# Two-layer decoder on one core: the first two queries of each cross-attention made in the stage ahead of it

## What is computed

```python
x = x + _L0_attn_ref(_layernorm(x), ...)            # softmax self-attention, 8 heads of 64
x = x + _L0_xattn_ref(_layernorm(x), ctx, ...)      # q = x Wq + bq, 16 heads of 16, softmax over 375 keys
x = x + _L0_ffn_ref(_layernorm(x), ...)             # top 2 of 8 experts, gelu, 1024 wide
x = x + _L1_attn_ref(_layernorm(x), ...)            # gated attention: norm again inside, silu, relu squared
x = x + _L1_xattn_ref(_layernorm(x), ctx, ...)      # norms x and the context with own gains and biases
x = x + _L1_ffn_ref(_layernorm(x), ...)             # top 2 of 8 experts, relu squared, 512 wide
```

## Time and profile before

| what | value |
|---|---|
| median of 3 runs | 2876.21 us (2872.34 to 2879.39) |
| profiled execution, its own time | 2876.75 us |
| its span | 2874.9 us |
| TensorE matmul busy | 2575.8 us, 90% of the span |
| VectorE busy | 1529.1 us, 53% |
| ScalarE busy | 1122.1 us, 39% |
| mean granted TensorE clock | 0.946 of full |

### The profile page before, as it was taken

The page is one execution under the profiler, slowest core; times in us unless marked ns, Lnnn a source line. Parts: engine busy times, 40 slices in busy tenths (PEclk is TensorE's granted clock), DMA queues, the critical chain, the costliest instruction groups (busy, mean ns, idle before and its releaser), DMA issues. The chain is left out here.

```text
span 2874.9 us, 57394 instructions
## 1 busy us (share of the span) xinstructions
PE 2575.8 (90%) x19210; PEld 2037.6 (71%) x19210; DVE 1529.1 (53%) x3357; ACT 1122.1 (39%) x2398; POOL 599.6 (21%) x652
## 2 busy tenths in 40 slices
PE   7999979789999975999999799899799999579992
PEld 4555555478888864888888566566688888468881
DVE  6777756456766664000000288455577777643334
ACT  2333345345555540333333244222455555312220
POOL 0000000023333310222222100000233333125542
PEclk9999999989999987999999899899899999779995
DMA  5110157777777732555555699000588888226666
GB/s 146 45 29 25 29 174 263 273 194 192 186 189 190 188 93 74 192 192 192 192 192 188 191 343 308 29 1 1 136 204 209 204 203 206 73 93 210 206 208 188
DMA packets 288417, 463.56 MB, mean 161 GB/s; under 512 B 75074, under 2 KB 216228, under 8 KB 288276
## 3 DMA queue, kind: packets, MB, share of 16 engines
q1 hardware_dynamic: 271508, 412.45, 50.3%
q0 software_dynamic: 16768, 49.30, 5.3%
HBM read 342.60 MB, written 119.02 MB: 161 GB/s over the span
## 5 line engine op out<-in xcount | busy, mean ns | idle before, releaser
L1444 ACT ACTIVATE x_probT<-banks 125x448 f32<-125x448 f32 x768 | 418.0, 544 | 382.9 <-PE banks L1341 372.8
L1544 DVE TENSOR_REDUCE x_neg_max<-banks 112x2 f32<-112x750 f32 x512 | 455.4, 930 | 93.4 <-PE banks L1325 93.4
L2103 PE MATMUL banks<-f_xT,f_w 128*128 128x256 f32 (+1 forms) x1680 | 369.9, 377 | 21.8 <-DMA f_b<-in_L_ffn_b 8.6
L2103 PEld LDWEIGHTS banks<-f_xT,f_w 128*128 128x128 f32 x1680 | 310.6, 197 | 74.9 <-issue 11.1
L1490 POOL TENSOR_TENSOR x_diag<-ident,x_neg_max 112x448 fp32r<-112x448 f32 x256 | 240.9, 941 | 581.6 <-DVE x_neg_max L1544 550.6
L2115 PE MATMUL banks<-f_w,f_hT 128*128 128x256 f32 x1584 | 355.8, 381 | 0.0
L1339 PE MATMUL banks<-x_diag,x_ones 112*125 112x448 f32 x768 | 324.0, 422 | 0.7 <-ACT x_probT L1444 0.6
L2115 PEld LDWEIGHTS banks<-f_w,f_hT 128*128 128x128 f32 x1584 | 297.7, 192 | 37.6
L1341 PEld LDWEIGHTS banks<-x_qP,x_kP 128*125 128x125 f32 x1536 | 290.5, 189 | 14.9
L1341 PE MATMUL banks<-x_qP,x_kP 128*125 128x224 f32 x1536 | 290.6, 271 | 0.0
L2162 DVE TENSOR_TENSOR f_y<-banks,f_b 128x256 f32<-128x256 f32 x66 | 25.1, 420 | 475.7 <-PE banks L2115 475.7
(11 more groups left out here) (331 smaller groups left out, 3789.1 us busy)
## 6 DMA issues: line engine op xcount, KB each, us to landing
x_kP<-k_halves SPq DMA_DIRECT2D x512, 188.0 KB, 3.6
f_w<-in_L_ffn_w SPq DMA_DIRECT2D x70, 1024.0 KB
f_w<-in_L_ffn_w SPq DMA_DIRECT2D x70, 512.0 KB
x_qP<-q_halves SPq DMA_DIRECT2D x512, 56.0 KB, 3.2
x_v<-v_rows SPq DMA_DIRECT2D x64, 408.0 KB, 3.2
k_halves<-p_halves SPq DMA_DIRECT2D x32, 752.0 KB, 4.5
k_halves<-f_d_halves SPq DMA_DIRECT2D x32, 752.0 KB, 6.4
q_halves<-x_q_halves SPq DMA_DIRECT2D x64, 224.0 KB, 2.3
```

The costliest lines, as they stand in the source:

```text
L1444: act.activation(probT[:, u % 2, c].rearrange("k h t -> k (h t)"), ST[i % 2][0:KB, 0:HU * T], ACT.Exp).then_inc(exp_done, 1)
L1544: dve.tensor_reduce(mx[:, u % RING, 2 * pair:2 * pair + 2], psum[0:T, 2 * pair:2 * pair + 2, 0:NKV], AX_X, ALU.max, negate=True).then_inc( ...
L2103: last = pe.matmul(bank[1 + f % 3][:, 0:width], w1[:, r, k, f * P:(f + 1) * P], xT[:, r, k, 0:width], start=(k == 0), stop=(k == KD - 1))
```

## The change

- The key stage's `KEYS` are four banks instead of two in layer 0, so that TensorE waits for VectorE's L1037 of the context two back (`least(2 * i + 2 - len(KEYS))`).
- `fold_pe` and the five bias additions go into the routing part of `experts(0)`; the nine weight scalings go one or two at a time ahead of VectorE's work of the last five expert tiles of layer 0.
- `first_queries` is new: it norms, turns, projects, splits and stores the queries of sequences 0 and 1 together. For layer 0 it stands in the key stage: factors and norm after context 26, TensorE's part behind the last context. For layer 1 it stands in `gated_attention`: factors of the two sequences and norm in group 4, TensorE's and ScalarE's part within the last group, VectorE's split ahead of the last group's `gated`.
- `cross_attention` starts its counters as if two queries had been made, and its opening loads keys and the stored queries at once. In layer 0 the norm factors are no longer made there.
- The two sets of norm factors of `gated_attention` are made at the end of layer 1's key stage.

```diff
@@ context_writer
     TURN, KEYS = (bank[0], bank[1]), (bank[2], bank[3])
+    if layer == 0:
+        KEYS = bank[0:4]
-        pe.wait_ge(k_low, ONE + 2 * i)
+        pe.wait_ge(k_low, ONE + least(2 * i + 2 - len(KEYS)))
@@ first_queries (new)
+    def norm(dve):
+        for b in range(2):
+            last = dve.tensor_scalar(xn[:, b, :], x[:, b, :], mv[:, b, 0:1], rstd[:, b:b + 1],
+                                     ALU.subtract, ALU.mult)
+    def turn(pe, to):
+        for k in range(KD):
+            for b in range(2):
+                last = pe.transpose(to[:, (2 * k + b) * T:(2 * k + b + 1) * T], xn[:, b, k * P:(k + 1) * P],
+                                    ident[0:T, 0:T])
+    def project(pe, to):
+        for m in range(KD):
+            for k in range(KD):
+                last = pe.matmul(to[:, m * TWICE:(m + 1) * TWICE], a.wqh[:, k, m, :], xnT[:, k, :],
+                                 start=(k == 0), stop=(k == KD - 1))
+    def store(sp):
+        sp.wait_ge(q_ready, 3)
+        for r in range(2):
+            sp.dma_start(e.q_halves[r].rearrange("h l p t -> p (h l) t"), ...).then_inc(stored, 16)
@@ project_context
             def _(pe):
                 for i in range(B):
                     c.tensor(pe, i)
-                    if i == FOLD:
-                        e.fold_pe(pe, wide_ready, folded_ps)
+                c.keys_read(pe, B - 2)
+                first.turn(pe, bank[0])
+                first.project(pe, bank[1])
...
-                        dve.wait_ge(folded_ps, 1)
-                        e.fold_dve(dve, fold_chain)
+                    if i == X_ASK:
+                        e.make_rstd_dve(dve, chain, x_std, x_asked, mv, rstd[:], e.norm_tmp, False, e.stat6)
+                        first.norm(dve)
+                first.split(dve, bank[1])
@@ cross_attention, SyncE
-                for half in range(2):
-                    load_keys(0, 0, half)
-                store_query(0, 0)
-                load_values(0, 0)
...
+                for s in range(2):
+                    load_keys(0, s, 0)
+                    sp.wait_ge(zeroed, s + 1)
+                    load_query(0, s)
+                    load_keys(0, s, 1)
+                    load_values(0, s)
@@ gated_attention
                 def project(g):
+                    if g + 1 == NG:
+                        pe.wait_ge(first.q_ready, 1)
...
+                    if g == NEXT:
+                        e.make_rstd_dve(dve, next_chain, std3, asked3, mv[:, 0:2], rstd[:, 0:2],
+                                        e.norm_tmp[:, :, 0:2], True, e.stat6[:, 0:2])
+                        first.norm(dve)
```

More of the change, by code:

```diff
@@ new lines, in decoder, with fold_weight @@
+        SCALES = 1 + 4 * KD
+        def fold_weight(dve, i, fold):
+            g = xa[1].gb
+            if i == 4 * KD:
+                fold(dve.tensor_scalar(xa[1].wv_twice[:], xa[1].wv_twice[:], g[:, 5:6], None, ALU.mult))
+                return
+            k, which = divmod(i, 4)
+            n = P if k == 0 else C1
+            if which == 0:
+                fold(dve.tensor_scalar(w.in_[:, k, :], w.in_[:, k, :], w.ln_gb[:, k:k + 1], None, ALU.mult))
+            elif which == 1:
+                wqh = xa[1].wqh[:, k].rearrange("c h n -> c (h n)")
+                fold(dve.tensor_scalar(wqh, wqh, g[:, k:k + 1], None, ALU.mult))
+            elif which == 2:
+                wkh = xa[1].wkh[:, k].rearrange("c h n -> c (h n)")
+                fold(dve.tensor_scalar(wkh, wkh, g[:, 4 + k:5 + k], None, ALU.mult))
+            else:
+                wv = xa[1].wv[0:n, k, :]
+                fold(dve.tensor_scalar(wv, wv, g[0:n, 4 + k:5 + k], None, ALU.mult))
@@ L1073, in _ @@
                 c.sync(sp)
+                first.store(sp)
                 c.stored(sp)
+                first.all_stored(sp)
             @block.gpsimd
@@ L1105, in _ @@
                         e.make_rstd_act(act, c_std, c_asked, ctmp)
+                    if i == X_ASK:
+                        e.make_rstd_act(act, x_std, x_asked, e.norm_tmp)
+                first.copy(act, bank[0])
             @block.vector
@@ L1412, in group @@
                             project(g, GROUP - 1)
-                for s in range(2):
-                    for j in MAKE:
-                        job(0, s, j)
                 pe.wait_ge(made, 2)
@@ L1476, in group @@
                             copy_oT(g, GROUP - 1)
-                for s in range(2):
-                    copy_xT(0, s)
                 for r in range(2, GROUP):
@@ L1592, in group @@
                             add_y(g, GROUP - 1)
-                for s in range(2):
-                    norm_x(0, s)
-                    split_q(0, s)
                 for u in range(AHEAD):
@@ L1804, in _ @@
                     pe.wait_ge(xT_ready, ONE + NG * KD)
+                    if layer == 0:
+                        e.fold_pe(pe, FOLD, fold_ps)
                     for n in range(2 * B):
@@ L2000, in _ @@
                     link(dve.tensor_copy(goes[:], spare[:]))
+                    if layer == 0:
+                        dve.wait_ge(fold_ps, 1)
+                        e.fold_biases(dve, FOLD, Chain(dve, fold_chain))
         xT = tile_sb("xT", [P, 2, KD, SLOTS])
@@ L2148, in _ @@
             def _(dve):
+                scale = Chain(dve, scaled)
                 def tile(n, i, r):
                     width = halves(n) * P
+                    if layer == 0 and type(n) is int:
+                        for j in range(2 * (n - PAIRED + 1), min(e.SCALES, 2 * (n - PAIRED + 2))):
+                            e.fold_weight(dve, j, scale)
                     if layer == 1:
@@ L2228, in _ @@
                     if layer == 0:
-                        e.residual_stats(dve, b)
+                        last = e.residual_stats(dve, b)
+                if layer == 0:
+                    last.then_inc(all_stats, 1)
+                    dve.wait_ge(all_stats, 1)
+                    factors = Chain(dve, pre2)
+                    e.make_rstd_dve(dve, factors, std1, asked1, mv, e.rstd_ga[:], e.norm_tmp, False, e.stat6)
+                    e.make_rstd_dve(dve, factors, std2, asked2, mv, rstd[:], e.norm_tmp, True)
 def gated_attention(e):
@@ L2268, in gated_attention @@
         tail = flag("tail")
+        NEXT = NG // 2
         def least(n):
@@ L2275, in gated_attention, with _ @@
         with nc.Block() as block:
+            @block.sync
+            def _(sp):
+                first.store(sp)
+                first.all_stored(sp)
             @block.tensor
@@ L2363, in _ @@
                         turn_in(g + 1)
+                    else:
+                        pe.wait_ge(y_read, ONE + g * GROUP)
+                        first.turn(pe, bank[0])
                     value(g, 2)
@@ L2504, in _ @@
                         queries_keys(g + 1)
+                    else:
+                        first.split(dve, bank[1])
                     for m in range(NE):
                         gated(g, m)
+                    if g == NEXT:
+                        next_chain = Chain(dve, next_pre)
+                        e.make_rstd_dve(dve, next_chain, std3, asked3, mv[:, 0:2], rstd[:, 0:2],
+                                        e.norm_tmp[:, :, 0:2], True, e.stat6[:, 0:2])
+                        first.norm(dve)
                     for s in range(GROUP):
```

149 lines of the change are left out of this document (92 added, 57 removed).

## The result

| | before | after |
|---|---|---|
| median of 3 runs | 2876.21 us | 2825.47 us (2824.13 to 2828.09) |
| profiled execution, its own time | 2876.75 us | 2828.09 us |
| its span | 2874.9 us | 2826.4 us |
| TensorE matmul busy | 2575.8 us | 2564.9 us |

The ratio is 0.983, with a 95% interval of 0.9815 to 0.9846: 1.7% faster. The prediction was 2828.

A forecast was written before the change was run, and what follows sets the result against it. TensorE was busy 90% of the span, so gains lay in its stalls and in work that could lie elsewhere. Terms -30, 0, +3.5, -10.2, -3.4, +3.0, -11.4 summed to -48.5 from 2876.75: forecast 2828 us, range 2818 to 2842.

The forecast's parts named there:

- Key stage, -30: Layer 0's key stage: removing the fold and adding two banks saves 30 us, bounds -32.4 to -13.3.
- The three kinds of loss: Key stage's 32.4 us lost: fold_pe near contexts 6 and 7, the hole after context 22, and remaining waits with lower-clock matmuls.
- kind (c): Key stage: 12.1 us of waits when finish or first factors held up VectorE, and lower-clock matmuls behind context 22's hole.
- the first rival: Key stage: stores pace it, by DMA rate or landing, so the kernel takes 2831 to 2845 us; chance 0.20.
- The estimate beside the forecast: Key stage: with HBM limited to about 358 GB/s, some 24 us come back in place of 30, 2834 in all.
- End of the key stage, +3.5: Border from key stage to stage 3: query work behind TensorE's end costs 3.5 us, bounds 0 to +6.
- Opening of stage 3, -10.2: First cross-attention: scores come 7.3 us after the stage's start instead of 17.5, saving 10.2 us.
- the second rival: Both cross-attention openings: other loads hold first scores or second key half 5 us each, kernel 2838 us; chance 0.12.
- The fold at 0: Routing and expert tiles of layer 0: the moved fold fits in TensorE's 18.78 us gap, costing 0, at worst +3.
- Gated attention's opening, -3.4: Border into gated attention: norm factors made before the stage begins save 3.4 us, range -1 to -4.
- Inside, +3.0: Gated attention: query transposes and products in the last group cost 2.1 us, VectorE work in group 4 costs 0.9.
- Opening of stage 6, -11.4: Second cross-attention: scores wait only for ones and query loads, 7.5 us after the start instead of 18.9, saving 11.4.

The follow-up runs named there:

- e1: Kernel after the change, but layer 0's key stage has two KEYS banks again instead of four: median 2838.35 us, ratio 0.9865 to before.
- e5: Kernel after the change, but layer 1's first two queries are made in the opening of cross-attention 1 (stage 6) again: median 2836.79 us.
- e6: Kernel after the change, but gated attention's two sets of norm factors are made at its opening again: median 2830.89 us.
- e7: Kernel after the change, but in both cross-attention openings ScalarE issues four of the first query load's eight DMAs, SyncE the other four: median 2827.26 us.
- e9: Kernel after the change, but layer 0's key stage leaves out the loads of contexts 4 to 31 and uses the first four again: median 2823.72 us.
- e11: Kernel after the change, but GpSimd copies the context's last 64 channels in SBUF instead of a second DMA loading them: median 2826.0 us.
- e8: Kernel after the change, but each context's keys of layer 0 are stored twice, 2.34 MB a context instead of 1.57: median 2884.85 us.
- e3: Kernel after the change, but layer 0's first two queries and x's norm factors are made in the opening of stage 3 again: median 2838.23 us.
- e12: Kernel after the change, with GpSimd's copy replacing the repeated context load and layer 0's first two queries made in stage 3 again: median 2831.07 us.

## Why the prediction was right, step by step

- **Key stage, -30: -31.4.** The three kinds of loss were the right ones, and "holes that cost a microsecond cost nothing" with four banks: in the kernel after no context behind `finish` or factors is longer than 4.47, save the two that VectorE's value copy held by 0.42 and 0.47. Measured alone, the fold gave 20.1 against its price of 13.3 and 6.99, and the banks 12.4 against the 12.1 of kind (c). The second agreement is in part luck: (c) held seven `finish` waits and some 2.8 us of lower clock behind the hole, e1 has nine such waits and no lower clock.
- **The argument for it was weaker than I took it.** "Because 368 has been seen at the full pace" was read as room above 353. Over 22 contexts the DMAs of the kernel after moved 338, at a share of 1.00 and a distance of 4.65 us; the 368 held for 5 us only. So the first rival had its mechanism right, stores that follow at 4.6 us or more, and what it had wrong is who pays: four banks let TensorE run ahead of the stores by 4 us more over the stage (10.3 against 6.4), and 32 contexts were few enough for that. The rest was paid at the end, 0.4 to 1.1 us in the stage and 0.5 to 1.9 at the border. The estimate beside the forecast from the 358 of the Trainium skill ("DMA: Bandwidth & Descriptors", Where 436 GB/s comes from) had it that lateness is hardly made up; here it grew. But the time of that estimate, 2834 with 24 us back in the stage, didn't come, as 31.4 came back. That the stage is short enough is nothing that the prediction worked out, so this part of its gain was won with luck.
- **End of the key stage, +3.5: +5.7, just inside its bound of 6** (+4.4 to +5.0 in e5, e6 and e7). Without the lag it measured 3.8 to 3.9 (e1, e9, e11), so the sum of the row prices was right and what was left out is the lag, which I had priced in the stage and not behind it.
- **Opening of stage 3, -10.2: -9.1.** The first query load was issued where forecast; the last step, "5.4 as now", took 6.5. That is the second rival's direction, at a fifth of its size, and no more than the old opening varies (17.5 to 18.7).
- **The fold at 0: 0**, with 5.00 us of the gap left though it ran at a granted clock of 0.62.
- **Gated attention's opening, -3.4: -2.8** (border 2.56 behind VectorE's end, not 1.9). The rows that its 5.5 us rest on are 20 operations, not 21. **Inside, +3.0: +1.2** (+1.0 to +2.3 over all kernels that keep this part): TensorE's products of the last group are there (0.55 + 1.68), but no wait of TensorE in group 4, for which I took 0.9. **Opening of stage 6, -11.4: -10.8** (-9.4 to -11.0).
- The sum of the terms came to -48.5 and the pieces to -47.2; the errors of +2.2, +1.1, +0.6 and +0.6 were offset by -1.4 and -1.8. That the profiled execution, 2828.09, lies 0.1 us from the 2828.2 of the sum is luck: single executions of this kernel differ by 4 us.

No kernel here beats the kernel after by more than the measurement can tell; e11 is 2.9 us shorter by its trace up to stage 3.

## What to carry to other kernels

When TensorE's waits are removed from a stage that also stores much, ask for the pace that the DMAs can keep and not only for TensorE's. The highest short stretch of a bandwidth column (368 over 5 us) says too much, and so does a kernel with a doubled store (360). The distance from one store's issue to the same store of the next context, over many contexts, tells it in the kernel itself: 4.65 us here, beside TensorE's 4.47. Extra PSUM banks let TensorE run over such a lag for as long as the stage is short enough, and then the lag is paid where the engines meet; so price it at the border. A wait that moves from one store to the other when a buffer is added speaks for a rate and not a landing time; that the DMAs never stand idle has to be seen as well.

## What I had not expected of the hardware

- A DMA share of 1.00 isn't one rate: it went with 338 GB/s in the kernel after (1.572 MB in 4.65 us), and 1.05 with 360 in e8 (2.342 MB in 6.50 us, more of it stores), with two buffers of the keys and with three.
- The landing of a 752 KB store does not follow the mean rate alone: from 440 to 530 the median is 3.6 us in e9 (274 GB/s, no loads), 4.7 before (281 GB/s), 5.0 after (338) and 7.5 in e8 (372).
- The end of a stage waits longer behind a full DMA queue: 7.4 us from the issue of the last store to the next stage in e3, 5.75 before and 5.7 in e12.
- GpSimd's copy of 64x375 floats to other partitions, once per context and 0.49 us each (e11), cost TensorE 2.3 us of weight-load waits and no time in the stage.
